# Turned inverse of levels 1 to 4 in a gated delta-rule block: VectorE 32x32-block transpositions in place of TensorE products and ScalarE copies

## The reference, cut to what matters

```python
q = _l2norm(hidden @ Wq); k = _l2norm(hidden @ Wk); v = hidden @ Wv
q, k, v = causal 4-tap convolution over time, then silu
beta = sigmoid(hidden @ Wb)
g = -exp(A_log) * softplus((hidden @ Wfa) @ Wfb + dt_bias)
def step(Sst, inp):
    qt, kt, vt, gt, bt = inp
    Sst = Sst * exp(gt)[..., :, None]
    err = vt - einsum('bhk,bhkv->bhv', kt, Sst)
    Sst = Sst + bt[..., None, None] * kt[..., :, None] * err[..., None, :]
    return Sst, einsum('bhk,bhkv->bhv', qt, Sst)
out = (rmsnorm(attn) * rms_scale * sigmoid(gate)) @ Wo
```

## Time and profile before

| | |
|---|---|
| median of 3 runs | 983.42 us (980.95 to 990.35) |
| span of the profiled execution, first to last instruction | 975.1 us |
| own time of the profiled execution | not given apart; median less span is 8.3 us |
| mean granted TensorE clock | 0.973 |

### The profile page before, as it was taken

How to read it: one execution, slowest core, us unless ns; L and a number is a source line. 1 busy time by engine, 2 the same in 40 slices (tenths; PEclk the granted TensorE clock), 3 DMA queues, 4 the chain that set the end, 5 groups by cost and what they waited for, 6 DMA issues and landing times.

```text
span 975.1 us, 53508 instructions
## 1 busy us (share of the span) xinstructions
PE 891.2 (91%) x24490; PEld 642.9 (66%) x24490; DVE 796.5 (82%) x1612; ACT 708.4 (73%) x1780; POOL 133.7 (14%) x307
## 2 busy tenths in 40 slices
PE   4889699999999999999999999899999998878886
PEld 4534356666677767777777667677776677667775
DVE  5577879888899989999999888799889999666424
ACT  3377758788888778888888788788878887555341
POOL 7000101111111101111111110111101111111000
PEclk9999889999999999999999999999999999998879
DMA  6100111100000111200001112000000000000001
GB/s 161 60 1 9 36 33 34 44 15 15 15 4 3 34 34 34 83 8 15 15 4 34 34 33 75 16 15 15 14 15 14 14 16 15 15 4 4 3 2 44
DMA packets 29110, 25.37 MB, mean 26 GB/s; under 512 B 4626, under 2 KB 24276, under 8 KB 28884
## 3 DMA queue, kind: packets, MB, share of 16 engines
q1 hardware_dynamic: 28884, 21.94, 8.1%
HBM read 20.82 MB, written 1.11 MB: 22 GB/s over the span
## 4 chain that ended last, share of the span: by engine, by line
PE 83%; DVE 7%; issue 4%; ACT 4%; POOL 2%; POOLq 0%; DVEq 0%; ACTq 0%
PE psum L893 17%; PE psum L951 13%; PE psum L926 6%; PE psum L1037 6%; PE psum L899 4%; PE psum L1015 3%; PE psum L1009 3%; PE psum L1002 3%; PE psum L988 3%; PE psum L995 3%; PE psum L908 3%; PE psum L903 3%; PE psum L933 2%; PE psum L962 2%; PE psum L978 2%
## 5 line engine op out<-in xcount | busy, mean ns | idle before, releaser
L893 PE MATMUL psum<-hT,gw 128*128 128x512 f32 x384 | 189.0, 618 | 0.8 <-ACT hT L554 0.8
L1332 DVE SCALAR_TENSOR_TENSOR qkv<-pad,chan,qkv 128x512 f32<-128x512 f32 x192 | 141.4, 776 | 0.1
L893 PEld LDWEIGHTS psum<-hT,gw 128*128 128x128 f32 x384 | 72.7, 196 | 89.3 <-issue 86.8
L1358 DVE TENSOR_TENSOR kq<-kq,tot 128x512 f32<-128x512 f32 x160 | 110.5, 691 | 22.8 <-PE psum L926 22.7
L1376 DVE COPY_PREDICATED pairs<-masks,psum 128x256 f32<-128x256 uint8 x192 | 101.8, 530 | 23.3 <-PE psum L926 14.1
L615 ACT ACTIVATE tmat<-psum 128x128 f32<-128x128 f32 x128 | 35.8, 280 | 94.1 <-PE psum L951 93.9
L951 PEld LDWEIGHTS psum<-fmat,pairs 32*32 32x32 f32 x4096 | 46.6, 107 | 60.8 <-issue 54.2
L623 ACT ACTIVATE rr<-rl 64x512 f32<-64x512 f32 x128 | 80.3, 627 | 1.7
L926 PE MATMUL psum<-kq,ks 128*32 128x32 f32 x5120 | 76.4, 200 | 2.5 <-issue 1.6
L610 ACT ACT_TABLE_LOAD x58 | 74.4, 1283 | 1.0
L1337 DVE SCALAR_TENSOR_TENSOR qkv<-pad,chan,qkv 128x512 f32<-128x512 f32 x96 | 72.2, 752 | 3.3 <-ACT qkv L655 3.3
(11 more groups left out here) (172 smaller groups left out, 1959.9 us busy)
## 6 DMA issues: line engine op xcount, KB each, us to landing
bb<-beta_rows SPq DMA_DIRECT2D x32, 256.0 KB, 3.4
gw<-in_L_attn_Wq SPq DMA_DIRECT2D x16, 128.0 KB, 2.3
gw<-in_L_attn_Wk SPq DMA_DIRECT2D x16, 128.0 KB, 2.4
gw<-in_L_attn_Wv SPq DMA_DIRECT2D x16, 128.0 KB, 2.3
gwo<-in_L_attn_Wo SPq DMA_DIRECT2D x4, 512.0 KB, 5.8
x<-in_L_attn_hidden_states SPq DMA_DIRECT2D x4, 256.0 KB, 4.4
gfb<-in_L_attn_Wfb SPq DMA_DIRECT2D x16, 64.0 KB, 2.2
ggb<-in_L_attn_Wgb SPq DMA_DIRECT2D x4, 256.0 KB, 5.0
```

What stands on the lines that cost most here:

```text
L893: last = eng.matmul(two(bank[to]), gw[:, t, kt, hh * D:(hh + 1) * D], two(hT[:, kt])[:, :, h * PW:(h + 1) * PW], start=(kt == 0), stop=(kt ...
L1332: last = eng.scalar_tensor_tensor(out=piece(t, i), in0=src, scalar=tap_weight(t, tap, i), in1=piece(t, i), op0=ALU.mult, op1=ALU.add)
L1358: eng.tensor_tensor(half(kq[:, p], h, 1), half(kq[:, p], h, 1), lower.rearrange("p (a n o) -> p a n o", a=1, o=1).broadcast_to((P, 2, nb, ...
```

## The change

VectorE gets a new function, `turn_inverse(p)`: one `transpose` instruction, which transposes each 32x32 block of the 128x256 tile `tmat`, leaves the blocks where they are in the grid, and writes `tt[:, p]`. It is called four times per chunk, each time after the ScalarE copy of natural level 1, 2, 3 or 4. The calls of `inverse_turned` and `copy_turned` for levels 1 to 4 are gone; level 5 stays. The waits move with them: TensorE's product of natural 2 waits for `turned1_ready`, natural 3 and 4 are covered by `summed3` and `summed4`, which come behind the transposition in VectorE's queue, and turned 5 waits for `turned4_ready`. ScalarE's whole-tile copy into `tmat` (L700) now waits for `turned4_ready` of the chunk before. Some waits that stood for the last or first slots only now stand for all.

```diff
-TT_BANK = (None, 7, 0, 6, 4, 2)
+TT_BANK = (None, None, None, None, None, 2)
...
 # GpSimd
-                    if n2 >= 27:
-                        after(turned4_ready, n2 + 1)
+                    after(turned4_ready, n2 + 1)
                     clear_turned(p).then_inc(turned_cleared, 1)
...
 # ScalarE
-                if 0 <= n1 < NCK:
-                    after(turned3_done, n1 + 1)
-                    copy_turned(q, 3).then_inc(turned3_ready, 1)
...
                     after(y5_done, n0)
+                    after(turned4_ready, n0)
                     eng.activation(tmat, bank[T0_BANK][:, 0:UC], ACT.Copy).then_inc(t0_ready, 1)
...
-                    after(turned4_done, n1 + 1)
-                    copy_turned(q, 4).then_inc(turned4_ready, 1)
...
-                if 0 <= n0 < NCK:
-                    after(turned1_done, n0 + 1)
-                    copy_turned(p, 1).then_inc(turned1_ready, 1)
...
-                    after(turned2_done, n0 + 1)
-                    copy_turned(p, 2).then_inc(turned2_ready, 1)
...
 # TensorE
-                if l < NL - 1:
-                    return block_products(o, l, fmat[:, l - 1], tt[:, p], 1)
...
-                    after(turned1_ready, im4 - 4)
+                    after(v_tapped, im4)
                     columns(im4, 2, V_BANK).then_inc(v_done, 1)
                 if 0 <= n1 < NCK:
                     after(us_ready, n1)
+                    after(turned1_ready, n1 + 1)
                     inverse_natural(q, 2).then_inc(natural2_done, 1)
-                    inverse_turned(q, 2).then_inc(turned2_done, 1)
                     if n1 <= 1:
                         after(decayed3, n1 + 1)
+                    if n1 <= 1:
+                        after(norm_ln, n1 + 6)
...
-                    after(turned2_ready, n2 + 2)
                     queries_state(p, n2).then_inc(os_done, 1)
...
-                    if n1 <= 0:
-                        after(turned2_ready, n1 + 1)
                     inverse_natural(q, 3).then_inc(natural3_done, 1)
...
-                    if n1 >= 31:
-                        after(kept4, n1 + 1)
-                    inverse_turned(q, 3).then_inc(turned3_done, 1)
+                    after(kept4, n1 + 1)
                     after(natural3_ready, n1 + 1)
                     inverse_y(4).then_inc(y4_done, 1)
...
                     after(ot_ready, n1)
-                    inverse_turned(q, 4).then_inc(turned4_done, 1)
...
                     inverse_y(2).then_inc(y2_done, 1)
-                    inverse_turned(p, 1).then_inc(turned1_done, 1)
...
 # VectorE
+            def turn_inverse(p):
+                return eng.transpose(tt[:, p], tmat)
...
                     inverse_sum(2).then_inc(summed2, 1)
+                    after(natural1_ready, n0 + 1)
+                    turn_inverse(p).then_inc(turned1_ready, 1)
                     decays(p, 3).then_inc(decayed3, 1)
...
                     decays(p, 4)
+                    after(natural2_ready, n0 + 1)
+                    turn_inverse(p)
                     after(y3_done, n0 + 1)
                     inverse_sum(3).then_inc(summed3, 1)
...
                     after(y4_done, n0 + 1)
+                    after(natural3_ready, n0 + 1)
+                    turn_inverse(p).then_inc(turned3_ready, 1)
                     inverse_sum(4).then_inc(summed4, 1)
...
-                        if n1 >= 31:
-                            after(sdec_ready, n1 + 1)
+                        after(sdec_ready, n1 + 1)
                         update_state(n1).then_inc(state_ready, 1)
...
                     decays(q, 1).then_inc(decayed1, 1)
+                if 0 <= n0 < NCK:
+                    after(natural4_ready, n0 + 1)
+                    turn_inverse(p).then_inc(turned4_ready, 1)
```

## The result

The changed kernel takes 942.97 us (median of 4 runs, 937.05 to 947.66) against 986.33 us before: ratio 0.960, 95% interval 0.9556 to 0.9644. In spans the gain is 975.1 - 943.3 = 31.8 us against the 16 forecast. The other 10 us or so between the medians lie in runs of before that were slower than its profiled one, and no profile of those is at hand.

The account below looks back on a forecast made before the run. It took TensorE to bound the main part, with VectorE 1.96 us per slot behind. Slots 6, pauses 6 and end 4 give 16 us off the 975.1 us span, so 959, plus 8.3 around it: 967; range 946 to 990.

Parts of the forecast that it names:

- The pauses: TensorE's 19.5 us of idle in 24 main-part slots: 3 us go with removed instructions, 3 more swallowed; 6 us gained.
- The 3 us for swallowing: Main part: where VectorE is the bound, TensorE's pauses are partly swallowed, as TensorE is slightly ahead; 3 us.
- The undisturbed slot: A main-part slot without disturbance: 25.05 us, 0.25 less than now, 6 us over 24 slots.
- The replay: One main-part slot followed operation by operation from the state update at 499.30, with each wait of VectorE, ScalarE and TensorE.
- The rival's own sum: ScalarE's wait at L700 delays its copies for TensorE; the slot's 0.25 us is given back: 977 us, chance 0.12.
- signs of "right": Transposition mean near 0.44 us, VectorE above 96% busy, TensorE gaps ended by VectorE or ScalarE, slot near 25.05, L700 released by VectorE.
- sign of "wrong": Transposition mean above 0.6 us, gapless TensorE slots of 24.2 us, or TensorE waiting mostly for ScalarE's L615 or L707.
- The floor of 0.27: Lower bound for one VectorE transposition of 128x256: 256 elements pass in 0.27 us.
- the rival of a dear transposition: Each VectorE transposition takes 0.7 us, making a slot 26.4 us and the kernel 1006 us; chance 0.15.
- 1.42 less 0.2 at natural 2: TensorE per slot: removing turned products 1 to 4 saves 1.42 us, 0.2 lost waiting for ScalarE's natural 2 copy.
- The end: Last 9 slots, bound by the chain through TensorE: 0.5 us net saved each, 4 us; bounds 0 and 11.
- The rival that had 943: TensorE stays the bound in the main part, a slot falls to about 24.2 us: 943 us, chance 0.15.

Follow-up runs that it names:

- before_equal: Before with the turned products of levels 1 to 4 each replaced by one matmul of 105 columns (24 at level 3): 961.04 us, ratio 0.981.
- turn_twice: After with a transposition of a constant tile added ahead of each of the four: 971.56 us, 0.997 of before.
- two_tmats: After with two `tmat` buffers by parity of the chunk, so ScalarE's copy waits for transposition 4 of two chunks back: 917.66 us, 0.939 of before.
- turn4_early: After with transposition 4 moved ahead of the next chunk's keep and level 1 decays, right behind the level 5 sum: 921.06 us, 0.937 of before.
- floor: two_tmats with each transposition replaced by a memset of one element: 914.41 us, 0.928 of before.
- before_wide: Before with the turned products of levels 1 to 4 each replaced by one wide matmul (213 columns, 152 at level 3): 973.87 us, ratio 1.000.

## Why the prediction was wrong, step by step

In spans the forecast gain was 16 us and the measured one 31.8. Of the 15.8 that are missing, 8.6 are pauses in the 24 slots, 3.8 the undisturbed slot, 2.9 the start and 0.5 the end.

- **The pauses: the step that failed.** "If pauses go with instructions that is 3 us ... 3 us more", with bounds 0 and 19.5. The idea that pauses go with instructions was right. The size was not: I let a sixth of the instructions take a sixth of the pauses, and they took five sixths (18.5 to 3.5 us). By the packets' times a pause comes only where the stream has used up what was there before the next packet arrives, so pauses fall by a multiple of the share removed. Measured 15 instead of 6. The 3 us for swallowing were a wrong reason: before_equal loses the same 15 with VectorE's load as before. Only the last 3.5 us can go that way (turn_twice, where TensorE waits for other things every slot, has none left).
- **The undisturbed slot.** Forecast 25.05, measured 24.85, 4 us over the 24 slots. "VectorE: 23.3 + 1.44 = 24.75 us of work" was too high: with no waits left, two_tmats shows 24.09, and turn_twice 25.50, four transpositions more. The missing 0.66 is spread over many operations that follow each other a little more closely; the five sums of the identity (`inverse_sum`) give the largest single share, 0.17 us. Beside it stands a loss of some 0.42 us that comes and goes. In before one small product of totals, 128x64, is in work together with a GpSimd operation on the same kind of tiles:

```profile
505.60 0.80 POOL L462 TENSOR_TENSOR tot<-dec 128x256 f32<-128x256 f32 x1 [9.48 <-ACT dec L723]
505.85 0.63 DVE L1363 TENSOR_TENSOR tot<-tot 128x64 f32<-128x64 f32 x1
```

It ends at 506.48, 0.08 us after GpSimd's. So do 22 of the 32 such products of before; the other ten take 0.21 to 0.22 us. In after 31 of the 32 come at another time and take 0.21 to 0.23 us, and the loss is gone. In two_tmats it is back, on another operation, the 128x256 product at L1346, which takes 0.40 us at other places:

```profile
599.25 0.70 POOL L462 TENSOR_TENSOR tot<-dec 128x256 f32<-128x256 f32 x1 [9.23 <-ACT dec L718]
599.40 0.83 DVE L1346 TENSOR_TENSOR ks<-ks,tot 128x256 f32<-128x256 f32 x1
```

So VectorE is held until GpSimd's operation is over. The thirteen traces have 207 such cases among these two groups of products; no run was made for it alone.
- **What bounds it.** "The bound moves to VectorE" was wrong. The three needs are 24.1 (VectorE), 24.1 (TensorE) and 24.85 (the loop from transposition 4 over ScalarE's copy to TensorE and back). I had this loop in the sum with about the right distances (output copy 0.85 us behind the copy into `tmat`, measured 510.06 - 509.26 = 0.80; level products 2 held to where they were) and named it as a rival, but priced it as an extra loss of 0.25 us against my sum instead of as the thing that the sum came from. The replay was right about when and wrong about who. The rival's own sum was wrong as well: with the 6 us of the slot given back, pauses (6) and end (4) remain, which is 983.4 - 10 = 973, not 977.
- **The signs.** Most of the signs of "right" came true: 128 transpositions with a mean of 443 ns, VectorE busy for 581.89 of 602.27 us (96.6%), L700 (now L697) released by VectorE. So did one sign of "wrong": TensorE waits mostly for ScalarE's L707 (now L704), 24 times. A busy share of 96.6% did not make VectorE the bound.
- **The transposition.** 0.36 us from start to start was forecast; 1.42 / 4 = 0.355 is what turn_twice shows against two_tmats and turn4_early (25.50 - 24.08), and 0.443 us is its duration. The floor of 0.27, the half rate of 0.7 and the rival of a dear transposition are out. The prediction took from the Trainium skill, "VectorE: DVE Perf Modes", section "The DRAIN you can't avoid", that the next operation starts only once the pipe is empty, and read it as a cost of the full duration. That reading is not borne out: 0.355 is less than 0.443. The same section adds, and the prediction left out, that a next operation that is not held starts earlier; with that the trace agrees.
- **TensorE's saving.** 1.42 less 0.2 at natural 2 was forecast, 24.1 us for TensorE alone; floor shows 24.08.
- **The end.** Forecast 4 us, measured 4.5, but this is luck. TensorE's pauses behind the 24 slots alone fell from 8.9 to 1.3 us, which the forecast did not have there. Against it the granted clock was lower in after, and TensorE waited more for VectorE's `keep_pairs` (9.2 us against 5.3). ScalarE waited up to 5.3 us for transposition 4, and TensorE only 1.1 us in all for that copy. The ends of before and after, 770.76 us and 743.47 us to the last instruction:

```profile
770.76:975.06 204.30, 171.93 (x5084) 139.92 (x5076) 133.97 (x297) 111.33 (x337) 22.68 (x46) 0.94 0.05 14
743.47:943.30 199.83, 169.69 (x4219) 136.76 (x4212) 141.33 (x323) 104.08 (x308) 22.27 (x46) 0.90 0.05 13
```

- **The start.** The 2.9 us ahead of the first solve were not forecast, and they are probably not of the change. The first solve comes at 140.5 to 145.7 us in the thirteen profiles, in no order that the edits explain. The four latest (143.8 to 145.7) are the four with a granted clock of 0.92 over this stretch, before among them; after had 0.94 and 141.2.
- **The base.** 8.3 us around the span should have been about 2. With it the forecast would have been 961, still 16 above the 945.35 us of the profiled run.
- **The range** took the pauses at 3 to 6 in every case and so ended above the result. The rival that had 943 (TensorE stays the bound) hit the number by accident: its slot of 24.2 us is that of two_tmats, not of after.

## What to carry to other kernels

A long unrolled stream of small matmuls can outrun its instruction supply, as here at 255 instructions in less than 3.3 us: look for idle time on TensorE that nothing releases and that ends just behind an instruction packet, and price instructions removed by the excess and not by their share. A transposition or copy that reads a single buffer holds the next writer; give that reader an early place in its queue, or the tile a second buffer, before judging which engine is the bound. To tell a bound from a loop that passes through an engine, add work to the engine: after lost 0.65 us for 1.42 us of added work, so 0.77 us of its slot were someone else's.

## What the runs showed of the hardware

- One packet of 16.4 KB on the queue `q8 instruction` per 255 TensorE instructions, never two within 3.2 us in the main part. Pauses of up to 1.9 us on TensorE where a slot of 25.3 us holds 768 recorded matmuls, hardly one where 25.5 us hold 642, and each ends 1.2 to 1.6 us after a packet.
- Of the VectorE products (128x64 totals, 128x256 `ks`) that start while GpSimd's 128x256 operation is in work, 207 of 342 over the thirteen kernels are held, and end 0.08 us (128x64) or 0.28 us (128x256) after it: 0.63 instead of 0.22 us, and 0.83 instead of 0.40.
- VectorE's transposition of 128x256 f32 in 32x32 blocks: 443 ns, 355 ns per further one; the product of two tiles of that size takes 416 ns.
- One f32 matmul of 213 columns (two records) takes 0.55 us among small ones, one of 152 columns 0.46 (517.53 to 517.99 in before_wide), while 16 matmuls of 32x32 blocks and 16 columns take 0.27 to 0.39.
